# Gate in two runs, feed-forward interwoven with the attention phase's tail and the next phase's lead steps

## The chip, the cores and the metric

The kernel runs on one core of a Trainium2 chip. The metric is the device time of one execution in microseconds (us), as the median of several runs. TensorE is the matmul engine, VectorE (DVE), ScalarE (ACT) and GpSimd (POOL) work on tiles, and the queue of SyncE (SP) issues nearly all DMAs.

## The reference, cut to what matters

```python
x = x + attention_a(layernorm(x))        # x: 32 items x 256 tokens x 128, 16 heads of 8
x = x + ffn(layernorm(x))
x = x + attention_b(layernorm(x))
x = x + ffn(layernorm(x))

def ffn(x, gate_w, down_w, down_b, up_w, up_b):
    pooled = x.mean(axis=1)                              # one row per item
    gate = softmax(pooled @ gate_w.T)                    # 8 experts
    top_w, top_i = top_k(gate, 2);  top_w /= top_w.sum() + 1e-8
    h = gelu(x @ down_w[top_i].T + down_b[top_i]) * top_w
    return sum over the two experts of (h @ up_w[top_i].T + top_w * up_b[top_i])
```

The gate of an item needs the mean over that item's tokens alone. Items never mix, neither in the attention nor in the feed-forward.

## The kernel before, in words

x stays in SBUF for the whole run (32 items of two 128-token tiles). There are four blocks in a row, each ended by all engines: attention a, feed-forward a, attention b, feed-forward b.

**Attention** is a pipeline over items. Step n (from -6 to 34) works on several items at once. With 8 slots p = 0..7 (pairs of heads) it does: statistics of item n+6 and of item n-2 on VectorE (L351, L360); the normalisation of items n+5 and n-3 on GpSimd (L326 to L335, transposed on TensorE in L582, copied on ScalarE in L463 and L465; the second is the input of the feed-forward, `normT`, with its sum over tokens in `pooled`); queries and keys of item n+4 (L546, L438 to L441), split into bf16 parts on GpSimd (L298 to L304), bounced through DRAM by SP (L289, L292); reading the stacks of item n+3 back from DRAM (L271, L273) and its values (L565, L450); scores for the row maximum of item n+2 (L504, `max_side`) with the maximum itself on VectorE (L379, `nmax`); scores again with the maximum subtracted for item n (L521, `exp_side`), the exponential on ScalarE (L418); the weighted values (L486, `weigh`; the fourth quarter belongs to the step after); for item n-1 the transposes, division, transposes and output projection (L429, L558, L395, L574, L456, L592), added to x in the next step (L368). A step does only what is live: steps -6 to -3 are light, steps -2 and -1 have no exponentials, steps 30 and 31 no `max_side`, and steps 32, 33 and 34 only carry the last items through their chains. One PSUM bank, `m_bank`, is shared by all the small products; `fill_m` makes TensorE wait for the last reader before each new use.

**Feed-forward** begins with the gate for all 32 items at once (L709 to L740): one matmul, then a serial chain of small VectorE instructions with one exponential on ScalarE and three visits to TensorE. SP moves the two chosen indices per item into `index`. Then items run in turn, n = -2..33: for item n+2 ScalarE and GpSimd copy the two chosen halves of the down weights (`wd`, L790, L694), ScalarE and VectorE scale the two halves of the up weights (`wu`, L792, L759); every four items each of these engines reads four expert numbers into registers; TensorE does down (L818) for item n, ScalarE the Gelu (L783), TensorE bias and up (L825, L833) for item n-2, and VectorE adds to x (L752). In feed-forward a the steps -6, -5, -4 and -3 of attention b are put between items, each as a whole, after items 13, 17, 21 and 25 of the emission; attention b then begins at step -2. In feed-forward b SP stores each item.

All order is fixed by hand: every engine has its own in-order instruction list, with semaphores between them.

Of the kernel before, what the change touches and what calls it, by code (L numbers as in the profile page):

```python
# [13 lines left out]
P = 128  # L14
# [38 lines left out]
def build(nc, x_dram_in, attn_w, attn_b, gate_w, down_w, down_b, up_w, up_b, tail_c, ident_c, iota_c, pick_c, out):  # L53
    ctx = ExitStack()
    with ctx:
# [61 lines left out]
        weight = sb("weight", [P, ITEMS])  # L117
        hotT = sb("hotT", [EXPERTS, TOP + 3, ITEMS])
        biasd = sb("biasd", [P, ITEMS])
# [4 lines left out]
        biasu_parts = sb("biasu_parts", [3 * ITEMS, WIDTH], BF16)  # L124
        pick = sb("pick", [3 * ITEMS, ITEMS], BF16)
        index = sb("index", [1, ITEMS * TOP], U32)
# [21 lines left out]
        banks = [ring[i][:, a, :] for i in range(3) for a in range(2)]  # L148
        t_bank, o_bank = banks[2:4], banks[4:6]
        values_bank = ctx.enter_context(nc.psum_tensor("values_bank", [P, 512], FP32))  # L150
        m_bank = ctx.enter_context(nc.psum_tensor("m_bank", [P, 512], FP32))

# [6 lines left out]
        with nc.Block() as block:  # L159
# [27 lines left out]
            @block.gpsimd  # L187
            def _(pool):
                nc.gpsimd.memset(minus_half[:, :, :], -0.5)
                for i in range(2):  # L190
# [10 lines left out]
        def attention(name, w, bias, masked):  # L201
# [29 lines left out]
            m_reader = [None]  # L231

            def one_step(emit, n):

                emit(n, n % RING, lambda k: 0 <= n + k < ITEMS, lambda k: (n + k) // 2)

            def steps(engine, emit, first):
                for n in range(first, ITEMS + BACK):
                    one_step(emit, n)
# [4 lines left out]
            def pair_of_scores(n, p):  # L244

                return ring[2 * (n * PAIRS + p) % 3]
# [8 lines left out]

            def sync_program(sp):

                sp.wait_ge(tail_in, 4 * 16 if masked else 2 * 4 * 16)

                def step(n, r, live, half):  # L260
# [34 lines left out]
            def gpsimd_program(pool):  # L295
# [10 lines left out]
                def step(n, r, live, half):  # L306
                    if live(1):
# [10 lines left out]
                    if live(5) or live(-3):  # L318
# [11 lines left out]
                        if norm_steps(n) > 2:  # L330
                            pool.wait_ge(xyT_done, norm_steps(n - 2))
                        for m, item in ((0, n + 5), (1, n - 3)):
# [5 lines left out]
                    if live(4):  # L338

                        i = (r + 4) % 2  # L340
                        pool.wait_ge(qk32_ready, (n + 4) + 1)
                        if live(2):
                            pool.wait_ge(bounced[(r + 2) % 2], half(2) * 96 + 96)
                        split(qk32[i][:, :, :], rest[i][:, :, :], parts[i][:, 0], parts[i][:, 1], parts[i][:, 2],
                              hi_ready, rest_done, mid_ready, parts_ready, n + 4)
                return step

            def vector_program(dve):
# [5 lines left out]
                def aggregate(n, item, i, m, raw_d, mv_d):  # L354

                    dve.wait_ge(raw_d, item + 1)
                    if norm_steps(n - 1) > 0:
                        dve.wait_ge(xy_ready, norm_steps(n - 1))
                    for t in range(TILES):
# [3 lines left out]
                def step(n, r, live, half):  # L363
                    if live(-2):
# [5 lines left out]
                    for p in range(PAIRS):  # L370
                        if live(2):

                            i = (r + 2) % 2
                            if p == 0 and live(0):
                                dve.wait_ge(mparts_ready, n + 1)
                            dve.wait_ge(s_done, (n + 2) * PAIRS + (p + 1))
                            src = pair_of_scores(n, p)[:, :, :].rearrange("p x (t k) -> p x t k", t=TILES)
                            dst = nmax[i][:, :, :].rearrange("p t (x j) -> p x t j", x=2)[:, :, :, p]
                            nc.vector.tensor_reduce(dst, src, axis=AX.X, op=ALU.max, negate=True).then_inc(max_done, 1)  # L379
                        if p == 2 and live(6):  # L380

                            for c, (start, _) in enumerate(CHUNKS):
                                if masked and n + 6 == start:
                                    dve.wait_ge(x_in[c], 16)
                            stats(n + 6, r % 2, raw_done)
                        if p == 3 and live(-1):

                            dve.wait_ge(on_done, (n - 1) + 1)
                            if live(-2):
                                dve.wait_ge(oT2_done, (n - 2) + 1)  # L390
                            both = m_bank[:, :].rearrange("p (m w) -> p m w", w=32)[:, :, 0:IN_SHARE * SUMS]
                            both = both.rearrange("p m (g e) -> p m g e", g=IN_SHARE)
                            nc.vector.reciprocal(rsum[:, :, :], both[:, :, :, HEAD]).then_inc(rsum_done, 1)
                            dve.wait_ge(rsum_done, (n - 1) + 1)
                            nc.vector.tensor_tensor(o[:, :, :].rearrange("p t (m g d) -> p (t m) g d", g=IN_SHARE, d=HEAD),  # L395
# [512 lines left out]
```

## Time and profile before

| what | value |
|---|---|
| median of 3 runs (lowest, highest) | 1039.98 us (1037.24, 1041.08) |
| profiled execution: own time, span of the trace | 1038.88 us, 1037.0 us |
| busy: TensorE, VectorE, ScalarE, GpSimd | 913.8, 788.4, 759.8, 595.9 us |
| mean granted TensorE clock, share of full | 0.965 |
| DMA traffic | 131.64 MB, 127 GB/s mean |

The span runs from the first to the last instruction of the trace. A busy time is the sum of an engine's instructions. Since the four blocks have different limits, the table says little on its own: the stretches between the attention steady states have to be read one by one.

### The profile page before, as it was taken

How to read it: one execution, taken by the hardware profiler on the slowest of the kernel's cores; microseconds unless marked ns; L12 is line 12 of the kernel's file. 1: busy time of each engine (PE TensorE's matmuls, PEld its weight loads, DVE VectorE, ACT ScalarE, POOL GpSimd, SP SyncE). 2: the span in 40 equal slices, each digit the busy share in tenths (PEclk: the TensorE clock that was granted, in tenths of full speed). 3: DMA queues.
4: the chain of work that ended last, by engine and by line, in shares of the span. 5: the costliest groups of instructions: out<-in, count | busy, mean ns of one | idle time of the engine just before them, and what ended most of it. 6: DMA issues, size and time to landing. Idle time of an engine off the chain costs nothing. (4 is left out here: it accounts for less than half of the span.)

```text
span 1037.0 us, 27550 instructions
## 1 busy us (share of the span) xinstructions
PE 913.8 (88%) x10204; PEld 519.3 (50%) x10204; DVE 788.4 (76%) x1398; ACT 759.8 (73%) x1324; POOL 595.9 (57%) x1011
## 2 busy tenths in 40 slices
PE   2379999999999999984876999999999999998577
PEld 1235555555555555442753455555555555554266
DVE  0388888888888888843448899899999999885244
ACT  1147888888888888783752888888888888888466
POOL 4555666666666666422355566666666666643211
PEclk9989999999999999997897999999999999999779
DMA  8545555455554544300035554544555545540023
GB/s 238 169 148 145 147 144 145 144 150 142 145 152 145 144 142 151 107 3 21 2 104 157 151 154 140 151 150 149 143 151 151 147 146 144 156 129 3 1 59 106
DMA packets 140516, 131.64 MB, mean 127 GB/s; under 512 B 9880, under 2 KB 121888, under 8 KB 140256
## 3 DMA queue, kind: packets, MB, share of 16 engines
q1 hardware_dynamic: 139312, 128.49, 42.6%
q8 instruction: 82, 1.34, 0.6%
q10 hardware_dynamic: 1072, 1.40, 0.5%
q14 instruction: 50, 0.41, 0.1%
HBM read 73.75 MB, written 55.57 MB: 125 GB/s over the span
## 5 line engine op out<-in xcount | busy, mean ns | idle before, releaser
L379 DVE TENSOR_REDUCE nmax<-ring 128x4 f32<-128x1024 f32 x512 | 607.8, 1217 | 74.1 <-PE ring L504 73.8
L418 ACT ACTIVATE probs<-ring 128x1024 f32<-128x1024 f32 x512 | 510.3, 1027 | 49.7 <-PE ring L521 46.4
L486 PE MATMUL values_bank<-probs,values 128*32 128x256 f32 x4096 | 274.1, 385 | 5.9 <-ACT probs L418 5.9
L504 PE MATMUL ring<-k_stack,q_stack 64*128 64x256 bf16 x2048 | 201.7, 278 | 42.9 <-DMA k_stack<-scratch 23.1
L335 POOL TENSOR_SCALAR xy<-x,mv,rstd 128x128 f32<-128x128 f32 x256 | 202.1, 800 | 8.7
L521 PE MATMUL ring<-q_stack,k_stack 64*128 64x256 bf16 x2048 | 187.4, 273 | 0.7 <-DVE nmax L379 0.4
L486 PEld LDWEIGHTS values_bank<-probs,values 128*32 128x32 f32 x4096 | 106.8, 109 | 90.4 <-issue 23.4
L298 POOL TENSOR_SCALAR mparts<-nmax 128x32 bf16<-128x32 f32 x64 | 13.9, 218 | 230.2 <-DVE nmax L379 230.2
L504 PEld LDWEIGHTS ring<-k_stack,q_stack 64*128 64x128 bf16 x2048 | 74.6, 95 | 139.0 <-ACT probs L418 67.3
L521 PEld LDWEIGHTS ring<-q_stack,k_stack 64*128 64x128 bf16 x2048 | 83.9, 95 | 75.4 <-issue 36.9
L450 ACT COPY values<-m_bank 128x128 f32<-128x128 f32 x128 | 29.0, 278 | 81.6 <-PE m_bank L565 81.6
L304 POOL TENSOR_TENSOR parts<-rest,parts 128x512 bf16<-128x512 f32 x64 | 74.4, 1162 | 5.3
L300 POOL TENSOR_TENSOR rest<-qk,parts 128x512 f32<-128x512 f32 x64 | 74.1, 1158 | 5.3
L368 DVE TENSOR_TENSOR x<-x,m_bank 128x256 f32<-128x256 f32 x64 | 26.9, 421 | 65.5 <-PE m_bank L592 65.5
L328 POOL TENSOR_TENSOR rstd<-varp,minus_half 128x4 f32<-128x4 f32 (+1 forms) x80 | 72.9, 911 | 6.7
L582 PE MATMUL m_bank<-ident,xy 128*128 128x128 f32 x256 | 47.3, 298 | 30.5 <-POOL xy L335 26.3
L351 DVE BATCH_NORM_STATS2 raw<-x 128x6 f32<-128x128 f32 x256 | 60.8, 279 | 15.0 <-PEq L159 14.9
L818 PE MATMUL ring<-normT,wd 128*128 128x256 f32 x128 | 45.1, 442 | 15.9 <-issue 7.7
L298 POOL TENSOR_SCALAR parts<-qk 128x512 bf16<-128x512 f32 x64 | 39.9, 624 | 27.2 <-ACT qk L439 17.9
L694 POOL COPY wd<-down_sb 128x64 f32 x64 | 14.7, 243 | 68.2 <-PE ring L818 52.0
L429 ACT COPY oT<-values_bank 128x512 f32<-128x512 f32 x64 | 37.5, 586 | 21.2 <-PE values_bank L486 21.2
L582 PEld LDWEIGHTS m_bank<-ident,xy 128*128 128x128 f32 x256 | 27.2, 144 | 48.7 <-POOL xy L335 18.5
(99 smaller groups left out, 1028.9 us busy)
## 6 DMA issues: line engine op xcount, KB each, us to landing
q_stack<-scratch SPq DMA_DIRECT2D x128, 256.0 KB
k_stack<-scratch SPq DMA_DIRECT2D x128, 256.0 KB
scratch<-parts SPq DMA_DIRECT2D x128, 192.0 KB, 2.5
scratch<-parts SPq DMA_DIRECT2D x128, 128.0 KB, 2.5
scratch<-parts SPq DMA_DIRECT2D x128, 64.0 KB, 3.1
out<-x SPq DMA_DIRECT2D x32, 128.0 KB, 1.8
q_stack<-maxT SPq DMA_DIRECT2D x128, 12.0 KB
scratch<-in_tail SPq DMA_DIRECT2D x8, 128.0 KB, 3.3
```

What stands on the lines that cost most here:

```text
L298: nc.gpsimd.tensor_scalar(hi, src, 1.0, 0.0, ALU.mult, ALU.add).then_inc(hi_done, 1)
L300: nc.gpsimd.tensor_tensor(tmp, src, hi, ALU.subtract).then_inc(rest_d, 1)
L304: nc.gpsimd.tensor_tensor(lo, tmp, mid, ALU.subtract).then_inc(lo_d, 1)
L328: nc.gpsimd.tensor_tensor(rstd[i][:, both, :], varp[i][:, both, :], minus_half[:, both, :], ALU.pow).then_inc(rstd_done, 1)
L335: last = nc.gpsimd.tensor_scalar(xy[i][:, m, t, :], x[:, item * TILES + t, :], mv[i][:, m, t, 0:1], rstd[i][:, m, t:t + 1], ALU.subtract, ...
L351: last = nc.vector.bn_stats(raw[i][:, t, :], x[:, item * TILES + t, :])
L379: nc.vector.tensor_reduce(dst, src, axis=AX.X, op=ALU.max, negate=True).then_inc(max_done, 1)
L418: nc.scalar.activation(probs[g % 2][:, c:c + 2, :, :], pair_of_exps(n, p)[:, :, :].rearrange("p x (k q) -> p x k q", k=TILES), ACT.Exp).th ...
L486: last = nc.tensor.matmul(values_bank[32 * c:32 * (c + 1), a * TOKENS:(a + 1) * TOKENS], values[item % RING][:, k, PER_GROUP * g + c, :], ...
L504: last = nc.tensor.matmul(pair_of_scores(n, p)[:, a, t * TOKENS:(t + 1) * TOKENS], q_stack[z][rows, p, t * P:(t + 1) * P], k_stack[z][rows ...
L521: last = nc.tensor.matmul(pair_of_exps(n, p)[:, a, k * TOKENS:(k + 1) * TOKENS], k_stack[r][rows, p, k * P:(k + 1) * P], q_stack[r][rows, ...
L582: last = nc.tensor.transpose(m_bank[:, at:at + P], xy[(r + 5) % 2][:, m, t, :], ident[:, :])
```

## The change

Each attention step can now be emitted slot by slot. The attention block ends after step 31. Steps 32, 33 and 34 are put between the items of the feed-forward that follows (`BEFORE`). The gate is computed in two runs: the first, for items 0 to 27, has its pieces between the slots of attention step 31; the second, for all 32 rows, of which items 28 to 31 are used, between the items 9 to 14 of the feed-forward (`GATE`). For the two runs `weight`, `biasd`, `biasu_parts` and `index` exist twice. The gate's products go to `m_bank` in place of the ring banks. Steps -6 to -2 of attention b are spread in pieces over items 8 to 32 of feed-forward a (`AFTER`); attention b then begins at step -1. The table of Gelu is no longer preloaded. The scores of steps before 0 use one ring bank pair (step -2 of b) or two (the others) where they used three. Three small memsets come into the set-up, and SP waits for the constant rows at step -3, not before the first step.

```diff
-            def sync_program(sp):
-                sp.wait_ge(tail_in, 4 * 16 if masked else 2 * 4 * 16)
+                    if n == -3:
+                        sp.wait_ge(tail_in, 4 * 16 if masked else 2 * 4 * 16)
...
-                return ring[2 * (n * PAIRS + p) % 3]
+                i = n * PAIRS + p
+                return ring[2 * i % 3 if i >= 0 else i % 2 if i >= SINGLE else 0]
...
+            SINGLE = -2 * PAIRS if masked else -PAIRS
...
-                    elif i - 3 >= -2 * PAIRS:
-                        pe.wait_ge(max_done, (i - 3) + 2 * PAIRS + 1)
+                    elif i < SINGLE and i - 1 >= -2 * PAIRS:
+                        pe.wait_ge(max_done, (i - 1) + 2 * PAIRS + 1)
+                    elif i != 1 and i - 2 >= max(SINGLE, -2 * PAIRS):
+                        pe.wait_ge(max_done, (i - 2) + 2 * PAIRS + 1)
...
+            def tensor_logits(pe):
+                fill_m(pe, dve_g, 1)
+                pe.wait_ge(yT_ready, rows)
...
+            def tensor_transposes(pe):
+                fill_m(pe, dve_g, HOT_T)
+                pe.wait_ge(dve_g, MIXED)
...
+            def tensor_biases(pe):
+                fill_m(pe, dve_g, BIASD + 1)
+                pe.wait_ge(dve_g, HOT_T)
...
+            programs = {"tensor": {1: tensor_logits, 5: tensor_transposes, 7: tensor_biases}, "scalar": {3: scalar_exps},
+                        "vector": {2: vector_best, 4: vector_top, 6: vector_weights, 8: vector_biases},
+                        "sync": {4: sync_index}, "gpsimd": {}}
...
+        EARLY = ITEMS - RING
+        def run(phase, first, gate):
+                for n in range(first, ITEMS):
+                    for p in range(PAIRS):
+                        phase["slot"](step, n, p)
+                        piece = gate["programs"][kind].get(p + 1)
+                        if n == ITEMS - 1 and piece:
+                            piece(engine)
...
+            BEFORE = {-2: (32, 0, 3), 0: (32, 3, 4), 1: (32, 4, 7), 2: (32, 7, 8), 4: (33, 0, 8), 7: (34, 0, 8)}
+            GATE = {9: (1, 2), 10: (2, 3), 11: (3, 4), 12: (4, 5), 13: (5, 7), 14: (7, 9)}
+            AFTER = {8: (-6, 0, 8), 10: (-5, 0, 3), 14: (-5, 3, 8), 15: (-4, 0, 3), 16: (-4, 3, 6), 17: (-4, 6, 8),
+                     18: (-3, 0, 3), 19: (-3, 3, 6), 20: (-3, 6, 8), 21: (-2, 0, 1), 23: (-2, 1, 2), 25: (-2, 2, 3),
+                     27: (-2, 3, 6), 30: (-2, 6, 7), 32: (-2, 7, 8)}
+            down_bank = [ring[2][:, i, 0:TOKENS] for i in range(2)]
+            up_bank = [values_bank[:, 0:TOKENS], ring[1][:, 0, 0:TOKENS]]
...
-                    nc.scalar.preload_act_table(ACT.Gelu)
...
-        run(phase_a, -6)
-        feed_forward("fa", False, phase_b)
-        run(phase_b, -2)
-        feed_forward("fb", True)
+        run(phase_a, -6, gate_a[0])
+        feed_forward("fa", phase_a, gate_a, phase_b, False, x_given[0])
+        run(phase_b, -1, gate_b[0])
+        feed_forward("fb", phase_b, gate_b, None, True, x_given[1])
```

## Rows read from the trace of the kernel before

**Rows 1.** Busy time in stretches: start:end, length, each engine's busy us, clock, DMA.

```profile
100.00:440.00 340.00, 332.42 (x4002) 182.98 (x4002) 300.55 (x490) 282.11 (x469) 224.65 (x363) 1.00 0.49 142
...
470.70:482.90 12.20, 4.58 (x32) 2.34 (x32) 3.00 (x12) 2.90 (x9) 4.98 (x8) 0.79 0.00 0
482.90:491.50 8.60, 1.91 (x14) 1.26 (x14) 5.06 (x27) 1.68 (x4) 0.76 (x4) 0.50 0.21 62
491.50:541.60 50.10, 41.38 (x242) 33.18 (x242) 22.12 (x81) 35.84 (x103) 21.47 (x48) 0.93 0.18 54
541.60:564.00 22.40, 12.17 (x86) 6.49 (x87) 19.83 (x25) 4.47 (x10) 13.53 (x23) 0.83 0.53 155
...
969.00:981.80 12.80, 5.54 (x32) 2.87 (x33) 2.70 (x12) 2.48 (x9) 4.98 (x8) 0.65 0.00 0
...
990.30:1034.80 44.50, 38.11 (x224) 31.02 (x224) 19.73 (x65) 33.10 (x96) 6.73 (x28) 0.93 0.31 90
```

**Rows 2.** Timeline, last step of attention a: start, length, engine, line, count, idle before.

```profile
464.90 0.39 PE L521 MATMUL ring<-q_stack,k_stack 64*128 64x256 bf16 x4
...
469.39 0.40 ACT L465 ACTIVATE normT<-m_bank 128x256 f32<-128x256 f32 x1
...
471.17 1.07 PE L486 MATMUL values_bank<-probs,values 128*32 128x256 f32 x16 [0.48 <-ACT probs L418]
472.30 0.59 ACT L429 COPY oT<-values_bank 128x512 f32<-128x512 f32 x1 [1.19 <-PE values_bank L486]
```

**Rows 3.** Timeline of gate a, from the exponential to the first weights.

```profile
484.25 1.28 ACT L773 ACT_TABLE_LOAD   x1
484.33 0.15 DVE L713 RECIPROCAL tsum<-esum 32x1 f32<-32x1 f32 x1 [0.53 <-ACT e L772]
...
487.20 0.18 PEld L800 LDWEIGHTS ring<-ident,wide 32*128 32x128 f32 x1 [4.05 <-DVE mix L726]
...
489.68 0.19 DVE L733 COPY biasd<-ring 128x32 f32<-128x32 f32 x1 [1.25 <-PE ring L808]
...
491.49 0.24 ACT L790 COPY wd<-down_sb 128x64 f32 x1 [5.96 <-DVE biasu_mid L737]
```

**Rows 4.** Timeline of ScalarE in feed-forward b: its start, and its steady state.

```profile
990.33 0.24 ACT L790 COPY wd<-down_sb 128x64 f32 x1 [5.99 <-DVE biasu_mid L737]
...
1001.62 0.24 ACT L790 COPY wd<-down_sb 128x64 f32 x1 [0.93 <-issue]
1001.89 0.40 ACT L792 ACTIVATE wu<-up_sb,weight 64x128 f32 x1
1002.31 0.47 ACT L783 ACTIVATE hT<-ring,biasd 128x256 f32<-128x256 f32 x1
```

**Rows 5.** Timeline around feed-forward a's end: lead steps of attention b.

```profile
527.18 0.70 PE L818 MATMUL ring<-normT,wd 128*128 128x256 f32 x2 [1.93 <-POOL wd L694]
...
532.03 0.45 ACT L450 COPY values<-m_bank 128x128 f32<-128x128 f32 x2 [0.80 <-PE m_bank L565]
...
542.77 3.49 DVE L379 TENSOR_REDUCE nmax<-ring 128x4 f32<-128x1024 f32 x3 [0.76 <-PE ring L504]
...
553.57 0.60 SPq L271 DMA_DIRECT2D q_stack<-scratch  x1
...
560.71 1.28 ACT L418 ACT_TABLE_LOAD   x1
...
564.02 0.61 PE L504 MATMUL ring<-k_stack,q_stack 64*128 64x256 bf16 x4 [3.41 <-DMA k_stack<-scratch]
...
565.09 1.02 ACT L418 ACTIVATE probs<-ring 128x1024 f32<-128x1024 f32 x1 [3.10 <-PE ring L521]
```

**Rows 6.** The page's groups: line, engine, operation, count, busy us, mean ns, idle before.

```profile
L335 POOL TENSOR_SCALAR xy<-x,mv,rstd 128x128 f32<-128x128 f32 x256 | 202.1, 800 | 8.7
...
L304 POOL TENSOR_TENSOR parts<-rest,parts 128x512 bf16<-128x512 f32 x64 | 74.4, 1162 | 5.3
...
L298 POOL TENSOR_SCALAR parts<-qk 128x512 bf16<-128x512 f32 x64 | 39.9, 624 | 27.2 <-ACT qk L439 17.9
```

More of the change, by code:

```diff
@@ L198, in _, with attention @@
                         nc.gpsimd.memset(of_group(r, g)[:, :, :, at:at + 1], 1.0)
-        def attention(name, w, bias, masked):
+        def attention(name, w, bias, masked, earlier=None, x_given=None):
             BACK = 3
@@ L229, in attention, with slot @@
             wq, wk, wv, wo = (w[:, i * WIDTH:(i + 1) * WIDTH] for i in range(4))
[L231 to L239, printed above, removed]
+            def slot(emit, n, p):
+                emit(n, p, n % RING, lambda k: 0 <= n + k < ITEMS, lambda k: (n + k) // 2)
             def tiles_of(item):
@@ L304, in split, with step @@
                     nc.gpsimd.tensor_tensor(lo, tmp, mid, ALU.subtract).then_inc(lo_d, 1)
-                def step(n, r, live, half):
-                    if live(1):
+                def step(n, p, r, live, half):
+                    if p == 0 and live(1):
                         i = (r + 1) % 2
@@ L361, in aggregate, with step @@
                     last.then_inc(mv_d, 1)
-                def step(n, r, live, half):
-                    if live(-2):
+                def step(n, p, r, live, half):
+                    if p == 0 and live(-2):
                         dve.wait_ge(wo_done, (n - 2) + 1)
@@ L604, in run, with steps @@
+        EARLY = ITEMS - RING
+        def run(phase, first, gate):
+            def steps(kind, engine):
+                step = phase["programs"][kind](engine)
+                for n in range(first, ITEMS):
[4 more added lines that the diff above has]
+                            piece(engine)
             with nc.Block() as block:
@@ new lines, in feed_forward, with of_item, steps @@
+            down_bank = [ring[2][:, i, 0:TOKENS] for i in range(2)]
+            up_bank = [values_bank[:, 0:TOKENS], ring[1][:, 0, 0:TOKENS]]
+            def of_item(item):
+                return gate_of[item >= EARLY], int(item >= EARLY)
+            def steps(kind, engine, emit):
+                old = before["programs"][kind](engine)
+                new = after["programs"][kind](engine) if after else None
+                for n in range(-AHEAD, ITEMS + BACK):
+                    if n in BEFORE:
+                        of_step, first, end = BEFORE[n]
+                        for p in range(first, end):
+                            before["slot"](old, of_step, p)
+                    for turn in range(*GATE.get(n, (0, 0))):
+                        if turn in gate_of[1]["programs"][kind]:
+                            gate_of[1]["programs"][kind][turn](engine)
+                    if after and n in AFTER:
+                        of_step, first, end = AFTER[n]
+                        for p in range(first, end):
+                            after["slot"](new, of_step, p)
+                    emit(n, n % RING, lambda k: 0 <= n + k < ITEMS)
@@ L835, in step @@
                             last.then_inc(up_done, 1)
-                    steps(pe, step, ahead_steps(pe, "tensor"))
+                    steps("tensor", pe, step)
                 @block.sync
                 def _(sp):
-                    sp.wait_ge(dve_g, WHICH)
-                    for k in range(TOP):
-                        sp.dma_start(index[0:1, k * ITEMS:(k + 1) * ITEMS], which[:, k:k + 1]).then_inc(index_in, 16)
-                    sp.wait_ge(index_in, 16 * TOP)
                     if not store:
@@ L856, in _ @@
+                    steps("sync", sp, step)
+                    if store:
                         sp.wait_ge(stored, 16 * ITEMS)
+        x_given = [sem("fa_x_ready"), sem("fb_x_ready")]
         phase_a = attention("a", wa, True, True)
-        phase_b = attention("b", wb, False, False)
-        run(phase_a, -6)
-        feed_forward("fa", False, phase_b)
-        run(phase_b, -2)
-        feed_forward("fb", True)
+        phase_b = attention("b", wb, False, False, phase_a, x_given[0])
+        gate_a, gate_b = ([gates(f"g{name}{i}", i, rows, phase["yT_ready"]) for i, rows in enumerate((EARLY, ITEMS))]
+                          for name, phase in (("a", phase_a), ("b", phase_b)))
```

588 lines of the change are left out of this document (300 added, 288 removed).

## The prediction

> **What bounds the kernel now.** I read the busy times in stretches first, and look for the stretches that are neither steady state. In the steady attention (100 to 440 us) TensorE is busy 332.42 of 340 us: that part is full, and the change leaves its instructions and their order alone [rows 1]. What lies between the two attentions, and behind the second, is not full. From 470.70 to 482.90 the three tail steps run with 4.58 us of TensorE and 2.90 us of ScalarE in 12.20; the gate takes 8.60 us with the clock at half speed; in feed-forward a ScalarE does 35.84 of 50.10 us; the lead steps -2 and -1 take 22.40 us, mostly VectorE [rows 1]. The same at the end: tail 12.80, gate about 8.5 (from 981.80 to the first weights at 990.33), feed-forward 44.50 [rows 1, 4]. The tail and the gate are chains of waits, one engine at a time, 42 us in all. That is what the change attacks.
>
> Then I read the timelines of these stretches, to see who sets the pace in each. In the feed-forward it is ScalarE: `wd`, `wu`, Gelu follow each other without a gap, 1.055 us an item by start to start, and each four items have a gap of 0.93 us for the expert numbers, so 5.27 us for four items [rows 4]. **Whatever ScalarE gets in addition in a feed-forward, lengthens it by that time.** GpSimd and VectorE have room there (feed-forward b: 6.73 and 19.73 us busy of 44.50 [rows 1]).
>
> **The attention's last step with the gate's first run.** The anchor is the last quarter of `weigh` for item 31, at 471.17, first work of step 32 before and after [rows 2]. Step 31 gets the gate's pieces in the in-order lists. The exponential of the gate stands behind those of slots 0 to 2 on ScalarE, and ends some 0.3 us after slot 4's scores (464.90 [rows 2]), at about 465.2. From there the VectorE chain to the last `mix` takes 487.17-484.33 = 2.84 us [rows 3], to 468.0. TensorE waits for it behind slot 4, and behind it stands the second quarter of `weigh`, which ran right after 464.90+0.8: with 0.6 us of transposes it comes about 2.9 us late, and so do slot 5's scores and ScalarE's exponentials of slots 5 to 7. Then the piece with the biases (turn 7) has to wait for the reader of `m_bank`, ScalarE's `normT` of that step, which stands behind the exponentials of slots 5 and 6 (469.39+0.40+0.2 before [rows 2], 3 us later now). Before, the third quarter of `weigh` and slot 7's scores ran during that time; now they follow it: biases 0.8 (between its half-clock row, about 1.2, and half of that), `weigh` 1.07, scores 0.4, exponential 1.0. Late in all: 5.1 us. Bounds: 2 (ScalarE's backlog covers most) and 8.
>
> **What goes.** From `weigh` to the first `wd`: before 491.49-471.17 = 20.3 us in a, and in b, where the same `weigh` opens the stretch at 969.0, 990.33-969.0 = 21.3 us [rows 1 to 4]. After: 5.1 late, `weigh` and semaphore 1.13, `oT` 0.59, then the expert numbers 0.93: 7.75 us. Gain 12.6 in a, 13.5 in b. What is late next is ScalarE itself.
>
> **What the feed-forwards get, both of them.** On ScalarE: `onT` 0.4, three `normT` at 0.4 with a read-out of 0.2 each, together 2.2 (from 469.39 [rows 2]); the second gate's exponential 0.4; table loads. The load of Gelu was hidden in the gate's chain (484.25 [rows 3]). Now the first Gelu brings it into the line, 1.28 us, of which 0.25 lie in the wait for the first down product: 1.0. The second gate's exponential brings two more, back and forth, 2.56. Waits: step 32's transposes and projection need each other's results at distances of one item, 0.8 us; TensorE waits at item 13 for the VectorE chain of 2.84 us, begun at item 11, and at item 14 for the copies behind it: 1.6 us beyond the two items that ScalarE is ahead. For the better: the clock. It stood at 0.50 in the gate and the first items of the feed-forward ran slowly [rows 1]; without the idle stretch they start at full clock, -1.0 us (bounds 0 and -2). Steps 33 and 34 have their GpSimd work (0.9+1.6 each [rows 6]) spaced by three items: hidden, and if not, up to 2 us each. Index and second weights are wanted only from item 26: hidden. Sum 2.2+0.4+1.0+2.6+0.8+1.6-1.0 = **7.6 us** for each feed-forward. Bounds 4 and 14.
>
> The Trainium skill (ScalarE: Activation LUTs, What ACT_TABLE_LOAD costs) gives about 1.28 us for the load and another 1.38 us for a drain with each switch of set. The load is the same here; for the drain no row speaks, since behind both loads ScalarE waits for others anyway. By that rule three switches would cost 4.1 us more in each feed-forward, and the sum would be 8 us worse.
>
> **What feed-forward a gets besides.** It took 50.05 us to the end of its items, b 44.0, so whole steps -6 to -3 cost 6 us now [rows 1]. After, steps -6 to -2: on ScalarE four `xnT` at 0.4, three `qk` at 0.6, two `values` at 0.45 [rows 5] = 4.2 us. On GpSimd each of steps -4 and -3 has 0.9+1.6 for the normalisation and 2 x 0.62+2 x 1.16 for the parts [rows 6], 6.3 us, and both now fall on items 15 to 20: 12.6 us and six `wd` at 0.4 make 15; ScalarE needs about 10 there, GpSimd is 2.3 ahead: 2.7 us late. That GpSimd can hold up the items, a row shows: 1.93 us at 527.18 [rows 5]. Step -2 has eight `nmax` of 1.16 us (3.49 for three [rows 5]) on VectorE, 9.3 us over items 21 to 32, with 0.7 of its own work for each item and the register reads: 22 us against ScalarE's 18.5; and since these scores have one bank pair, slots 3 to 5, emitted together at item 27, let TensorE wait for two `nmax` in a row, some 3 us. The two overlap: 4 us. Together 10.9, less 6 = **4.9 us more**. Bounds 1 and 12.
>
> **The lead steps after it.** Before, 22.40 us from the block's start to step 0, of which step -1 began at 551.6; the end of that time is set by a DMA: the reads for item 2 were issued at 553.57 and the scores had them at 564.02, 10.4 us later [rows 1, 5]. After, step -2 is gone from here, item 2's parts are ready before the feed-forward ends, and SP issues that read at once. It then lands at +0.8+10.4 = 11.2 us from the end of feed-forward a; VectorE's step -1, eight `nmax` and statistics, needs 10.1 and, with two bank pairs where there were three, 0.8 more, and one us of starting. I take 13.2 (0.8 block start, 11.6, 0.8), bounds 11.2 and 16. Gain 22.5-13.2 = **9.3 us**. At the start of attention a the two pairs cost the same 0.8, largely under the waits for the reads: 0.5. Memsets and the moved wait of SP: nothing, they lie under the loads of the first 14 us.
>
> **Sum.** a: 12.6-7.6-4.9+9.3 = 9.4. b: 13.5-7.6 = 5.9. Start -0.5. Together 14.8 us. The profiled execution had 1037.0 us of span and 1.9 around it, 1038.88; it becomes 1024.1. The median shown is 1.1 higher: **1025 us**. Steady attention and final store are taken as unchanged.
>
> **Rivals.** *A, better hidden.* The late 5.1 in step 31 is mostly covered, as ScalarE has exponentials in hand, and step -2 fits beside the items. With the lower bounds (2 for 5.1 twice, 5 for 7.6 twice, 1.5 for 4.9): 15 us more, 1010. For: every engine but ScalarE has room. Against: the lists are in order, and TensorE's waits stand in front of work that ScalarE needs.
> *B, the waits multiply.* Each wait for `m_bank` inside the feed-forward stops TensorE, ScalarE runs dry, and it adds to ScalarE's own time instead of overlapping. Both feed-forwards at 13 for 7.6, a's further 4.9 at 12, step 31 at 8 for 5.1 twice: 10.8+7.1+5.8 = 24 us less gain, so 1049, slower than before. It decides from some 15 us beyond my sum on. For: one lead step now brings waits of 1.93 us (TensorE, 527.18) and 0.80 (ScalarE, 532.03) [rows 5]. Against: pieces are small and set apart.
> *C, about half of B*: 12 of those 24 us are lost, 1037.
> *D, a switch of the table costs more than its row.* Its upper bound is the 3.1 us that pass between the load's end at 561.99 and the next exponential [rows 5], which waits for scores there. At half of it, 1.5 us for each of the six loads, 9 us: 1034. For: no row has work waiting behind a load. Against: the load at 560.71 starts without a pause. The skill's rule above is this case, at 1033.
> *E, the change does not do what it says.* The items of the feed-forward are held by the tail's chains, since the steps 32 to 34 stand in the same in-order lists, ahead of items 0 to 7: the tail is moved and not hidden. Then 12.2+12.8 us come back, less the 2.2+0.8 charged for them twice: 19 us, 1044. Against: the pieces lie one to three items apart, and their longest part, 2.5 us of GpSimd, is shorter.
>
> **Chances.** Forecast (1016 to 1032) 0.55; A 0.2; D 0.07; C 0.08; E 0.03; B 0.07. The range takes A's centre and goes to C: 1009 to 1038. A difference of 0.5% (5.2 us) is about what this measurement can tell from none: faster 0.82 (forecast, A, D), same 0.11 (C, E), slower 0.07 (B).
>
> **What would show it.** Right: the last `weigh` of item 31 about 5 us behind its old place with TensorE waits for `mix` and for `normT` in step 31; first `wd` some 8 us behind 471; three table loads in each feed-forward with 1.28 us between ScalarE's items; feed-forwards of about 52 and 61 us from first `wd` to last up; step 0 of b about 13 us after feed-forward a. Wrong: a first `weigh` delay under 3 us, no gap for the loads, item gaps at 15 to 20 and at 27 missing, or a wait for the stacks of item 1 or 2 longer than before.

## The result, and the profile after

| | before | after |
|---|---|---|
| median (lowest, highest), 4 runs each | 1040.33 us (1037.24, 1041.08) | 1052.32 us (1050.28, 1055.79) |
| ratio, 95% interval | | 1.0133 (1.0116 to 1.015) |
| profiled execution: own time, span | 1038.88, 1037.0 us | 1050.78, 1048.9 us |
| mean granted clock | 0.965 | 0.964 |

The kernel became 12 us slower where 15 us of gain were forecast. The time lies outside the range, and beside rival B (1049). Chips differ a little (the kernel before has medians from 1038.78 to 1040.33 us below), so each experiment is compared with the runs of the kernel before that were made beside it.

First the busy times in stretches of the kernel after (start:end, length, each engine's busy us with its instructions, clock, DMA). They are cut by stage, finer than [rows 1]:

```profile
61.00:463.00 402.00, 386.77 (x4643) 211.12 (x4642) 344.72 (x557) 329.12 (x538) 252.97 (x412) 1.00 0.47 136
463.00:478.60 15.60, 10.86 (x111) 5.29 (x105) 6.28 (x32) 8.46 (x14) 0.02 (x1) 0.78 0.01 1
...
481.30:492.60 11.30, 7.09 (x26) 5.42 (x26) 2.98 (x13) 7.13 (x19) 4.10 (x12) 0.70 0.07 20
492.60:502.50 9.90, 8.96 (x60) 7.43 (x61) 6.07 (x27) 8.14 (x25) 5.76 (x12) 1.00 0.01 2
502.50:519.70 17.20, 12.05 (x56) 9.21 (x55) 8.88 (x40) 9.18 (x23) 4.47 (x13) 0.70 0.01 1
519.70:528.80 9.10, 6.62 (x44) 5.40 (x43) 6.50 (x17) 6.91 (x22) 8.57 (x15) 1.00 0.40 120
528.80:562.40 33.60, 21.80 (x129) 15.86 (x129) 17.70 (x34) 12.18 (x36) 9.12 (x19) 0.80 0.35 102
562.40:572.90 10.50, 5.88 (x45) 2.73 (x46) 9.74 (x15) 2.97 (x6) 6.95 (x12) 0.86 0.51 155
...
1010.00:1025.30 15.30, 10.32 (x49) 7.77 (x49) 7.98 (x35) 8.24 (x21) 1.19 (x5) 0.67 0.17 48
1025.30:1046.10 20.80, 18.11 (x119) 15.07 (x117) 9.84 (x31) 15.88 (x47) 2.85 (x12) 1.00 0.34 99
```

The reader sees two kinds of stretch. Where attention is in its steady state (61 to 463) nothing is lost, and little where only items run, or items with light pieces: 492.6 to 502.5 and 1025.3 to 1046.1 hold the full clock (1.00) with ScalarE busy for about four fifths; from 519.7 to 528.8 the clock is full too, and GpSimd has no room left (8.57 of 9.10). In the others, step 31 (463.0 to 478.6), the first items with step 32, the items with the second gate (502.5 to 519.7 and 1010.0 to 1025.3) and the items with step -2 (528.8 to 562.4), TensorE is busy for 63 to 70% and the clock is at 0.67 to 0.80. Idle time that stood in one block before is now cut up and placed among the work.

The change, from piece to piece (starts in the two traces):

| piece | before | after | forecast | measured |
|---|---|---|---|---|
| start, attention a | | | +0.5 | +1.04 |
| last `weigh` of item 31, a | 471.17 | 478.58 | +5.1 | +6.4 |
| from it to the first `wd` | 20.32 | 2.73 | -17.7 | -17.6 |
| feed-forward a, to the last up product | 50.06 | 81.09 | +12.5 | +31.0 |
| from there to step 0 of b | 22.5 | 10.5 | -9.3 | -12.0 |
| attention b up to step 31 | | | 0 | +0.9 |
| last `weigh` of item 31, b | 969.14 | 985.51 | +5.1 | +6.6 |
| from it to the first `wd` | 21.19 | 3.35 | -18.6 | -17.8 |
| feed-forward b | 43.98 | 57.28 | +7.6 | +13.3 |

Measured, they give 11.9 us, which is 1048.9-1037.0. Of the 1.04 us at the start 0.72 stand already at the first matmul (19.24 against 18.52 us); experiments below with the same set-up have it between 18.57 and 19.34, so that part is no effect of the change. What was to go went; what came instead was too much, 18.5 us of it in feed-forward a and 5.7 in b. Where inside: I counted the start of each item's Gelu from the first `wd`. In b the difference grows at a few places only:

| Gelu of item | before b | after b | after a |
|---|---|---|---|
| 0 | 1.6 | 2.9 | 2.7 |
| 5 | 8.8 | 13.9 | 14.1 |
| 10 | 15.1 | 20.7 | 20.8 |
| 15 | 22.8 | 36.0 | 37.9 |
| 20 | 29.1 | 42.3 | 47.1 |
| 26 | 36.5 | 49.7 | 66.5 |
| 27 | 38.6 | 51.8 | 74.7 |
| 31 | 42.7 | 56.0 | 79.6 |

In b: 1.3 for the table load, 3.8 more up to item 5 (step 32), 0.5 up to item 10 (steps 33 and 34, hidden as forecast), 7.6 from 10 to 15 (the second gate), then nothing. In a the same, and from item 15 on 41.7 us where b takes 20.0; the gap before item 21 alone is 9.2, that before item 27 is 8.2.

The waits of TensorE in feed-forward a (line waited at, who released it, us in total, times, longest):

```profile
PE ring L521 <- DMA k_stack<-scratch: 6.5, 1, 6.5
PE ring L521 <- DVE nmax L399: 4.1, 2, 2.8
PE m_bank L637 <- DVE mix L685: 3.8, 1, 3.8
PE m_bank L598 <- ACT onT L477: 3.0, 1, 3.0
```

All but that for `nmax` (two) are single waits, with TensorE's whole queue behind it. In the timeline (start, length, engine, line, tiles, count, and the idle time before):

```profile
469.18 0.22 PE L637 MATMUL m_bank<-ident,wide 32*128 32x32 f32 x1 [2.72 <-DVE mix L685]
...
473.71 0.42 PE L648 MATMUL m_bank<-hotT,downb_sb 8*64 8x32 f32 x4 [1.35 <-ACT normT L486]
...
474.73 1.94 PE L501 MATMUL values_bank<-probs,values 128*32 128x256 f32 x16
...
477.25 1.02 ACT L439 ACTIVATE probs<-ring 128x1024 f32<-128x1024 f32 x1 [3.59 <-PE ring L538]
...
504.04 1.28 ACT L654 ACT_TABLE_LOAD   x1
505.34 0.30 ACT L654 ACTIVATE e<-logit,nbest 32x8 f32<-32x8 f32 x1
505.55 0.18 ACT L654 ACTIVATION_READ_ACCUMULATOR e<-logit,nbest 32x1 f32 x1
505.75 1.28 ACT L858 ACT_TABLE_LOAD   x1
507.04 0.47 ACT L858 ACTIVATE hT<-ring,biasd 128x256 f32<-128x256 f32 x1
...
508.72 0.28 PE L637 MATMUL m_bank<-ident,wide 32*128 32x32 f32 x1 [3.79 <-DVE mix L685]
...
509.20 1.22 PE L880 MATMUL ring<-normT,wd 128*128 128x256 f32 x2
...
511.59 0.47 ACT L858 ACTIVATE hT<-ring,biasd 128x256 f32<-128x256 f32 x1 [2.46 <-PE ring L900]
...
525.24 0.69 SPq L279 DMA_DIRECT2D q_stack<-scratch  x1
...
534.72 0.61 PE L521 MATMUL ring<-k_stack,q_stack 64*128 64x256 bf16 x4 [6.46 <-DMA k_stack<-scratch]
535.25 1.22 PE L880 MATMUL ring<-normT,wd 128*128 128x256 f32 x2
...
537.64 0.47 ACT L858 ACTIVATE hT<-ring,biasd 128x256 f32<-128x256 f32 x1 [8.26 <-PE ring L900]
```

Read it from TensorE's wait to ScalarE's: `mix` holds TensorE for 3.79 us, and ScalarE then idles for 2.46, and for 1.22 and 1.61 more in the two items behind; the stacks hold TensorE for 6.46, and ScalarE idles for 8.26. The price is that of ScalarE. At the stacks it is more than TensorE's wait, because the matmuls behind that wait run at half clock: the down products at 535.25 take 1.22 us for two, as at 509.20 behind `mix`, against 0.70 at 527.18 [rows 5]. In step 31 `weigh` takes 1.94 us at 474.73 against 1.07 [rows 2].

### The profile page after: what moved, and what is told of

Its sections match the earlier page's. It is cut to its first block and busy times, and to the rows that moved or that the text cites. A ratio compares the mean times of both kernels' runs of the same rounds, so it can differ in the third digit from the quotient of the medians.

```text
span 1048.9 us, 27756 instructions
## 1 busy us (share of the span) xinstructions
PE 929.5 (89%) x10232; PEld 528.0 (50%) x10232; DVE 803.3 (77%) x1452; ACT 765.9 (73%) x1332; POOL 594.7 (57%) x1014
## 5 line engine op out<-in xcount | busy, mean ns | idle before, releaser
L501 PE MATMUL values_bank<-probs,values 128*32 128x256 f32 x4096 | 277.2, 388 | 3.4 <-ACT probs L439 2.7
L306 POOL TENSOR_SCALAR mparts<-nmax 128x32 bf16<-128x32 f32 x64 | 13.9, 218 | 233.6 <-DVE nmax L399 227.2
L334 POOL TENSOR_SCALAR varp<-mv 128x4 f32<-128x4 f32 (+1 forms) x80 | 15.7, 197 | 71.4 <-POOLq L734 39.2
L880 PE MATMUL ring<-normT,wd 128*128 128x256 f32 x128 | 48.5, 466 | 7.0 <-issue 4.2
```

The costliest lines, as they stand in the source:

```text
L501: last = nc.tensor.matmul(values_bank[32 * c:32 * (c + 1), a * TOKENS:(a + 1) * TOKENS], values[item % RING][:, k, PER_GROUP * g + c, :], ...
L880: nc.tensor.matmul(down_bank[r % 2], wd[r][:, :, :].rearrange("p a b -> p (a b)"), normT[:, n, :], start=True, stop=True).then_inc(down_do ...
```

## The experiments

Each kernel is the one after with the edit shown, or an experiment before it with one edit more. W is the theory that waits of TensorE in the in-order lists make the loss. "After, a / b" below are the lengths of feed-forward a and b in the trace, 81.09 and 57.28 in the kernel after. Feed-forward b is the same code in that kernel and in e1, e2 and e4, and has 57.28 to 58.95 there: such a length is good to about 1.7 us.

| label | median us (runs) | kernel before, us | ratio, 95% | a / b |
|---|---|---|---|---|
| e1_lead2_out | 1046.52 (5) | 1038.87 | 1.0082 (1.0054 to 1.0111) | 63.65 / 57.50 |
| e2_lead2_late | 1044.44 (5) | 1038.87 | 1.0062 (1.0041 to 1.0082) | 71.74 / 58.95 |
| e3_gate2_none | 1036.57 (10) | 1038.87 | 0.9978 (0.996 to 0.9996) | 71.95 / 49.64 |
| e4_gate1_at6 | 1044.39 (5) | 1038.87 | 1.0054 (1.0032 to 1.0077) | 81.08 / 57.84 |
| e6_gate2_noexp | 1049.91 (4) | 1040.01 | 1.0109 (1.0082 to 1.0137) | 80.26 / 56.0 |
| e7_gate2_spaced | 1047.86 (4) | 1040.01 | 1.0083 (1.0062 to 1.0104) | 79.98 / 54.78 |
| e9_all_late | 1031.16 (4) | 1040.01 | 0.9926 (0.9904 to 0.9948) | 69.26 / 53.67 |
| e10_before_spaced | 1023.46 (4) | 1040.01 | 0.984 (0.982 to 0.9861) | 64.75 / 51.21 |
| e11_preload_moved | 1019.45 (5) | 1038.78 | 0.982 (0.9803 to 0.9837) | 64.75 / 49.64 |
| e12_lead2_out_all | 1023.81 (4) | 1038.78 | 0.9859 (0.9844 to 0.9874) | 55.91 / 49.98 |
| e13_exp_earlier | 1019.73 (5) | 1038.78 | 0.9821 (0.9807 to 0.9836) | 64.61 / 49.82 |

**Step -2 out of the feed-forward (e1_lead2_out).** It runs at the start of attention b as before the change, with the three bank pairs.

```diff
-                     18: (-3, 0, 3), 19: (-3, 3, 6), 20: (-3, 6, 8), 21: (-2, 0, 1), ... 32: (-2, 7, 8)}
+                     18: (-3, 0, 3), 19: (-3, 3, 6), 20: (-3, 6, 8)}
-        run(phase_b, -1, gate_b[0])
+        run(phase_b, -2, gate_b[0])
-                return ring[2 * i % 3 if i >= 0 else i % 2 if i >= SINGLE else 0]
+                return ring[2 * (n * PAIRS + p) % 3]
```

> Step -2 of attention b is taken out of feed-forward a and runs whole at the start of attention b, as before the change; the scores of steps before 0 have three bank pairs again. The rest is the changed kernel (1052.3 us; span 1048.9). Theory W (in-order waits): in the changed kernel items 21 to 33 of feed-forward a take 34 us where bare items take some 15, so the step costs 19 there and saves 12 behind it. Without it: feed-forward a some 62 us from first wd to last up (81 in the changed kernel), lead steps 22 us again, first step of a 1 us earlier: 1052.3-7-1 = 1044 us. Rival V (volume: the step's work costs what it costs wherever it stands): feed-forward a shorter by just the 12 us that come back behind it, 1051 us.

Feed-forward a is 17.4 us shorter, and the way from its last up product to the next exponential is 24.1 us, where it was 11.8. Net 4.2 us of span. So step -2 inside cost more than it saved. What is left of feed-forward a is 6.2 us longer than b (63.65 and 57.50), as in the kernel before (50.06 and 43.98, 6.1 us): spreading steps -6 to -3 cost nothing more in sum, and step -2 is what made feed-forward a so much longer than b.

**Step -2 at the end of it (e2_lead2_late).** The slots stand behind items 26 to 33, one each.

```diff
-                     18: (-3, 0, 3), 19: (-3, 3, 6), 20: (-3, 6, 8), 21: (-2, 0, 1), 23: (-2, 1, 2), 25: (-2, 2, 3),
-                     27: (-2, 3, 6), 30: (-2, 6, 7), 32: (-2, 7, 8)}
+                     18: (-3, 0, 3), 19: (-3, 3, 6), 20: (-3, 6, 8), 26: (-2, 0, 1), 27: (-2, 1, 2), 28: (-2, 2, 3),
+                     29: (-2, 3, 4), 30: (-2, 4, 5), 31: (-2, 5, 6), 32: (-2, 6, 7), 33: (-2, 7, 8)}
```

> The same instructions as the changed kernel; step -2's eight slots stand at items 26 to 33, one each, in place of items 21, 23, 25, 27 (three), 30, 32. Theory W: TensorE's 6.5 us wait for the stack of item 0 (and the half clock behind it) goes, since the read lands some 5 items earlier than wanted; the two waits for nmax at item 27 go as well, but VectorE has eight nmax of 1.2 us in eight items of 1.3: some 3 us come back. 1052.3-6 = 1046 us; no wait of TensorE for k_stack in feed-forward a. Rival V: the volume of VectorE and ScalarE sets the time, no change or slower by 1 to 3 us (all of it crowded at the end), 1052 to 1055 us.

The waits of TensorE from 480 to 552 in its trace:

```profile
PE m_bank L637 <- DVE mix L685: 3.8, 1, 3.8
PE m_bank L598 <- ACT onT L477: 3.0, 1, 3.0
PE ring L521 <- DVE nmax L399: 2.4, 5, 1.2
```

The wait for the stacks is gone, that for `nmax` is 2.4 us in five pieces, feed-forward a is 9.35 us shorter, and the step is still inside. From the Gelu of item 20 to that of item 21 it is 1.1 us where it was 9.2, to that of item 27 5.2 where it was 8.2. The first slot stands 5 items later and the three slots of item 27 stand apart; the work is the same: the place was most of the fault. Against e1 the step still costs 8.1 us inside. The waits for `mix` and `onT` stand as they were.

**The second gate left out (e3_gate2_none).** Items 28 to 31 take the experts and weights of items 24 to 27, so that part of the computation is missing.

```diff
-            GATE = {9: (1, 2), 10: (2, 3), 11: (3, 4), 12: (4, 5), 13: (5, 7), 14: (7, 9)}
+            GATE = {}
+            col = lambda i: i if i < EARLY else i - RING
```

> The second run of the gate is left out in both feed-forwards; items 28 to 31 take the experts and weights of items 24 to 27 (that part of the computation is changed). Theory W: five items with the gate take 15.3 us in feed-forward b where bare ones take 7.1, and about as much more in a: 8 us each, 1052.3-16 = 1036 us, first wd at the same place. Rival P (the prediction's price, 0.4+2.6+1.6 each): 1052.3-9 = 1043 us.

Both feed-forwards are shorter, by 9.1 and 7.6 us. The 7.6 us in b are just what the table of Gelu starts had between items 10 and 15. The wait for the stacks stays (7.6 us where it was 6.5). This kernel is also where a second gate that costs nothing would end, at about the time of the kernel before.

**The first gate's visits to TensorE joined (e4_gate1_at6).** Transposes and biases both stand behind slot 5, one slot later than the transposes stood and one earlier than the biases.

```diff
+            if run_of == 0:
+                programs["tensor"] = {1: tensor_logits, 6: tensor_both}
+                programs["vector"] = {2: vector_best, 4: vector_top, 6: vector_both}
```

> Only the first run of the gate is moved inside attention step 31: its transposes come behind slot 5 (were behind slot 4), its biases right behind them (were behind slot 6, waiting for normT); VectorE's pieces follow. Theory W: TensorE issues weigh and scores of slot 5 before it waits, so ScalarE keeps working; the wait for normT is gone. The last weigh of item 31 comes 2 us late in place of 6.4 and 6.6: 1052.3-9 = 1043 us. Rival: the gate's chain itself has to fit into the step and only changes place, last weigh still 5 to 6 us late: 1051 us.

The last `weigh` comes at 472.98 in a (478.58 in the kernel after), and at 975.58 in b (985.51): 5.6 us in a and 4.3 more in b. Of the 6.4 us that step 31 was late, 0.8 are left.

**No table loads for the second gate (e6_gate2_noexp).** ScalarE copies the logits where it took their exponential, so the weights of items 28 to 31 are others.

```diff
-                nc.scalar.activation(e[of_run, :], logit[of_run, :], ACT.Exp, bias...
+                nc.scalar.activation(e[of_run, :], logit[of_run, :], ACT.Identity if run_of else ACT.Exp, bias...
```

> The changed kernel with the second gate's exponential replaced by a plain copy with bias on ScalarE (the gate of items 28 to 31 is computed wrongly): same instructions and waits, but no load of the Exp table and none back to Gelu in the feed-forwards. Leaving the second gate out altogether gave 7.6 us in feed-forward b and 9.1 in a. Theory W: two loads of 1.28 us each are in ScalarE's line, the rest is TensorE's wait for the VectorE chain (3.8 us) with the half clock behind it; the chain starts 1.3 us earlier: some 2.6 to 3.5 us less in each feed-forward, 1052.5-6 = 1046 us. Rival D (a switch costs more than its row, 2.8 us each): 5.5 us or more less in each, 1041 us.

Two loads of 1.28 us gone in each feed-forward, and they are shorter by 0.8 and 1.3 us only, less than such lengths can tell. Its timeline shows the reason:

```profile
504.95 0.30 ACT L654 ACTIVATE e<-logit,nbest 32x8 f32<-32x8 f32 x1
...
505.38 0.15 DVE L671 RECIPROCAL tsum<-esum 32x1 f32<-32x1 f32 x1
...
507.97 0.21 DVE L685 SCALAR_TENSOR_TENSOR mix<-hot,wt,mix 32x8 f32<-32x8 f32 x1
508.33 0.28 PE L637 MATMUL m_bank<-ident,wide 32*128 32x32 f32 x1 [2.51 <-DVE mix L685]
...
511.20 0.47 ACT L858 ACTIVATE hT<-ring,biasd 128x256 f32<-128x256 f32 x1 [3.90 <-PE ring L900]
```

The chain on VectorE, 2.8 us from 505.38 to 508.18, sets when TensorE goes on. ScalarE's Gelu of item 13 starts at 511.20 in place of 511.59; the loads had lain mostly beside that chain, and ScalarE idles for 3.90 us where it idled for 2.46. My size for W (1046) missed, and D, which asked for 5.5 us or more in each, is refuted.

**The second gate's last pieces later (e7_gate2_spaced).**

```diff
-            GATE = {9: (1, 2), 10: (2, 3), 11: (3, 4), 12: (4, 5), 13: (5, 7), 14: (7, 9)}
+            GATE = {9: (1, 2), 10: (2, 3), 11: (3, 4), 12: (4, 5), 15: (5, 7), 18: (7, 9)}
```

> The changed kernel with the second gate's last pieces later: transposes and weights at item 15 (were 13), biases at item 18 (were 14). Nothing is left out. Theory W: TensorE no longer waits 3.8 us for mix and keeps its clock, ScalarE's table loads stay: about 4 of 8 us come back in each feed-forward, 1052.5-8 = 1044 us. Rival V (volume of the gate's instructions on VectorE and ScalarE): 0 to 2 us, 1051 us. In a the pieces fall among steps -4 and -3, so less may come back there.

1.1 us less in a and 2.5 in b, of the 9.1 and 7.6 that the second gate costs: the value lies between the two expectations. TensorE's wait for `mix` is gone, 3.8 us in each. In b a wait of 2.8 us for ScalarE's `wd`, behind the two table loads, has come in its place; in a there is one too, and the stacks still hold TensorE for 4.5 us. So this wait was partly beside work of ScalarE, and only the part beyond came back.

**All three, and the load of Gelu's table at the end of the attention (e9_all_late).** e2, e4 and e7 together, and one line:

```diff
+                if kind == "scalar":
+                    nc.scalar.preload_act_table(ACT.Gelu)
```

> Three edits together: step -2's slots at items 26 to 33 (alone -8 us), first gate behind slot 5 (alone -8), second gate's last pieces at items 15 and 18; and in addition the Gelu table is preloaded at the end of the attention blocks, behind the last exponential, where ScalarE waits for weigh anyway. Theory W: the waits are separate and add up: 1052.5-8-8-8-2.6 = 1026 us, faster than before by 13. Rival: behind each wait the next one comes forward (table loads, GpSimd's parts, VectorE's nmax), half of it stays: 1037 us.

The spans of e2, e4 and e7 lie 7.9, 10.3 and 4.6 us under that of the kernel after. Added, they give 1026.1; e9 has 1028.3. The trace of e4 is its fastest run, 4 us under its median; by the medians (7.9, 7.9 and 4.5 under 1052.32) the sum is 1032.0, and e9 has 1031.16. The savings add up, within some 2 us, and the load added nothing to them: what it gives in the feed-forward (the first Gelu 1.6 us behind `wd` where it was 2.7) goes at the block's end, where it stands last on ScalarE and all engines wait for it.

```profile
475.45 1.28 ACT L744 ACT_TABLE_LOAD   x1
...
477.03 1.07 PE L501 MATMUL values_bank<-probs,values 128*32 128x256 f32 x16 [1.72 <-PEq L746]
```

That wait is 0.73 us in e4, which has the same step 31 and no load (0.40 in the kernel after, whose step 31 ends otherwise).

**Step 32 spaced out (e10_before_spaced).** Each piece of step 32 that uses another's result stands an item later, and steps 33, 34, the gate and step -6 one item later too.

```diff
-            BEFORE = {-2: (32, 0, 3), 0: (32, 3, 4), 1: (32, 4, 7), 2: (32, 7, 8), 4: (33, 0, 8), 7: (34, 0, 8)}
+            BEFORE = {-2: (32, 0, 3), 0: (32, 3, 4), 1: (32, 4, 6), 2: (32, 6, 7), 3: (32, 7, 8), 5: (33, 0, 8), 8: (34, 0, 8)}
-            GATE = {9: (1, 2), 10: (2, 3), 11: (3, 4), 12: (4, 5), 15: (5, 7), 18: (7, 9)}
+            GATE = {10: (1, 2), 11: (2, 3), 12: (3, 4), 13: (4, 5), 16: (5, 7), 19: (7, 9)}
```

> As the kernel with all edits, with the attention's tail further apart in the feed-forward: step 32's slots 6 and 7 one item later each, step 33 at item 5 (was 4), step 34 at 8 (was 7), the gate's pieces and step -6 one item later. Theory W: TensorE waits 3.0 us for onT at item 1 since ScalarE has the Gelu load and item 0 first; the preload and the distance take 2 to 3 us from each feed-forward: 2 to 4 us below the kernel with all edits, 1023 us. Rival V: no difference between the two.

It brought 7.7 us of the medians against e9, more than was expected of the step alone: 4.5 in feed-forward a, 2.5 in b. In a the first Gelus start at 1.6, 3.1, 5.0, 7.1 and 8.1 us, where e9 had 1.6, 4.8, 7.7, 9.8 and 12.0. Up to item 5, where only step 32 differs, it is 2.6 us in a and 3.0 in b; the rest of the gain belongs to the other pieces that moved.

**The load moved to the start of the feed-forward (e11_preload_moved).** It is ScalarE's first instruction there.

```diff
                     experts = [None]
+                    nc.scalar.preload_act_table(ACT.Gelu)
```

> As the kernel with the spaced tail (1023.5), but the Gelu table is loaded as the first instruction of ScalarE in each feed-forward block, not as the last of the attention block. In that kernel TensorE waits 2.0 us at the block's start before the last weigh (0.40 in the changed kernel), as all engines end the block together and ScalarE's load of 1.28 us belongs to it. Theory: behind the start it lies in ScalarE's wait for that weigh, so the weigh comes 1.3 us earlier in each phase and hT(0) stays 1.6 us behind the first wd: 1021 us. Rival: the load pushes oT by what weigh gained, no difference, 1023.5 us.

```profile
463.00:473.10 10.10, 7.16 (x87) 3.35 (x85) 6.17 (x30) 7.17 (x13) 0.00 (x0) 1.00 0.01 2
475.85:540.60 64.75, 49.80 (x310) 38.46 (x310) 39.90 (x127) 42.22 (x118) 32.41 (x69) 0.95 0.26 74
```

```profile
473.10 1.28 ACT L859 ACT_TABLE_LOAD   x1 [0.28 <-PEq L744]
...
473.13 1.07 PE L501 MATMUL values_bank<-probs,values 128*32 128x256 f32 x16 [0.73 <-PEq L744]
...
474.39 0.59 ACT L450 COPY oT<-values_bank 128x512 f32<-128x512 f32 x1
...
475.85 0.24 ACT L876 COPY wd<-down_sb 128x64 f32 x1 [0.88 <-issue]
```

The load lies under the last `weigh`, and costs nothing: the first `wd` stands 2.72 us behind that `weigh`, 2.73 in the kernel after, which has no load there. The clock is 1.00 from 463 us to the end of step 31 and 0.95 over feed-forward a, where the kernel after had 0.78 and 0.81. This version beats both kernels: 1019.45 us, 1.8% under the kernel before (0.9803 to 0.9837), with the same pieces in other places and the load ahead of the first items. The 4.0 us under e10's median are not all the load's: against the kernel before, e10 has 0.982 to 0.9861, which overlaps. The traces show TensorE's wait at the two block ends shorter by 1.3 and 0.9 us (2.02 and 1.51 in e10, 0.73 and 0.56 here). The rest is not explained; e10's step 31 in a ran at 0.87 where this one has 1.00.

**Step -2 out again, from the good version (e12_lead2_out_all).** e11 with the edit of e1.

```diff
-                     18: (-3, 0, 3), 19: (-3, 3, 6), 20: (-3, 6, 8), 26: (-2, 0, 1), ... 33: (-2, 7, 8)}
+                     18: (-3, 0, 3), 19: (-3, 3, 6), 20: (-3, 6, 8)}
-        run(phase_b, -1, gate_b[0])
+        run(phase_b, -2, gate_b[0])
```

> As e11, but step -2 of attention b whole at the start of attention b, and three bank pairs for all scores before step 0. Tells whether the step is worth its place in the feed-forward once it is set late. Theory W: with late slots it still costs some 10 us in the feed-forward (VectorE's eight nmax) and saves 12 behind it; and the three pairs give 1 us back at the start: within 2 us of e11, 1020 to 1023 us. Rival (the overlap of step -2 is where the gain is): 10 us slower, 1031 us.

Feed-forward a is 8.8 us shorter, and the way to the next exponential is 23.1 us instead of 12.4. So step -2 inside now costs less than it saves, 1.7 us of span and 4.4 of the medians, where it had cost 4.2 more than it saved in the kernel after. That is more than the first expectation allowed (1023) and far from the rival (1031).

**The first gate's exponential earlier (e13_exp_earlier).** e11 with that piece behind slot 1 instead of slot 2.

```diff
+                programs["scalar"] = {2: scalar_exps}
```

> As e11, with the first gate's exponential one slot earlier on ScalarE (behind slot 1 of step 31, was behind slot 2). VectorE's chain then begins behind its own division of slot 3 instead of behind the exponential, some 0.4 to 0.7 us earlier. Theory W: TensorE's wait for mix and all behind it shrink by that, 0.5 us in each phase, 1020 us. Rival: no difference to e11, since VectorE is what the chain waits for.

1019.73 against 1019.45: no difference that this can tell. The edit hardly moved the chain: from the logits' matmul to `wide`, the first matmul behind `mix`, it is 6.83 us in a and 6.73 in b, where e11 has 6.88 and 6.87. An earlier end of the chain was therefore not tried; the exponential was not what held it.

## Why the prediction was wrong, point by point

- **From `weigh` to the first `wd`**: right, 2.73 and 3.35 us for 2.65. The tail and the gate did leave their place, so rival E (not hidden at all) is out: steps 33 and 34 cost at most 0.5 us together.
- **Step 31**: right in kind and near in size. Both waits that were named are there (2.72 for `mix`, 1.35 for `normT`), and 6.4 us late for 5.1. The part missing is the clock: `weigh` behind them took 1.94 us, where the sum had 1.07.
- **The load of the table**: 1.28 us, and no more. ScalarE's items stand right behind it (505.75 and 1.28, next start 507.04), at all six loads. D's mechanism does not exist here. The Trainium skill (ScalarE: Activation LUTs, What ACT_TABLE_LOAD costs) gives about 1.28 us for the load, as measured, and 1.38 us more for a drain, which none of these six loads shows.
- **The lead steps after feed-forward a**: right in its mechanism, 10.5 us for 13.2, and 0.7 under the lower bound. SP issued the read for item 2 at 563.39, 1.0 us behind the last up product (562.40), and the scores had it at 572.90, 9.5 us later where the sum took 10.4 and 1.2 more for VectorE.
- **What the feed-forwards get, 7.6 each**: wrong, 13.3 in b. Step 32 was priced at 0.8 us of waits, and 1.0 of ScalarE's own for `onT` and a `normT`, and cost 3.8 up to item 5. The second gate was priced at 0.4+2.6+1.6 = 4.6 and cost 7.6. That "they start at full clock, -1.0 us" did not come: over the first 11.3 us of feed-forward a the clock was 0.70, as in the kernel before, here behind the waits of steps 31 and 32.
- **Feed-forward a's further 4.9 us**: the step that failed. It measured 31.0-13.3 = 17.7, the largest miss of the sum (12.8 us). The prediction priced step -2 by VectorE's work and two `nmax` waits, and never asked when the stacks of item 0 would be there: it put that wait at nothing. Slot 0 of step -2 stands at item 21, the read's issue was at 525.24, three items ahead, and the scores had it at 534.72: 9.5 us. Moving the step later took 8.1 us out of this one gap (e2), and with the step out altogether feed-forward a is 17.4 us shorter (e1). A row for such a read was at hand, 10.4 us from issue to scores [rows 5], and I used it for item 2 after the feed-forward only.
- **The rule behind all of these**: the prediction took a wait of TensorE as lying beside ScalarE's work ("the two items that ScalarE is ahead"). At the stacks ScalarE went on for only 1.1 us after TensorE had stopped (529.39 against 528.26), and behind a wait TensorE needs longer for each item than ScalarE does: from 487.83 to 489.75 the down products came 1.92 us apart at half clock, against 1.055 of ScalarE [rows 4]. So that wait was paid in full and a little more: from the kernel after to e2 the waits for stacks and `nmax` fall by 8.2 us, and feed-forward a by 9.35. The wait for `mix` was not: of its 3.8 us in b, e7 got 2.5 back, since ScalarE had two table loads beside it. This was rival B, given 0.07; its 13, 12 and 8 us stand against 13.3, 17.7 and 6.4 measured, so that its 1049 is near partly because its misses offset. Rival A's 1010 is no sum of the stated lower bounds: it takes 5 and 1.5 us where they are 4 and 1, and with those it would be 1008, outside the range.

What was shown: step -2's places, which hold the stacks' wait and that for `nmax` together (e2), the second gate (e3), the two visits in step 31 (e4), step 32's distances up to item 5 (e10) and the end-of-block load (e9 against e11), each by its own kernel. What the half clock alone adds in the feed-forwards was not separated. For the end of step 31, e11's two phases do it: from the start of the second bias matmul to the next block the same instructions take 4.27 us in a, at a clock of 1.00, and 5.59 us in b, at 0.69. There the clock alone is 1.3 us.

## What to carry to other kernels

Interweaving a chain with in-order work pays only if every piece stands so far behind what it needs, a DMA's landing and another engine's chain included, that the shared engine does not wait; here the same pieces gave +1.3% or, in other places and with one table load ahead of the items, -1.8%. Price a wait of the shared engine at its full length plus the slower items behind it, and take off only what the pacing engine is shown to have of its own to do there, as the table loads here. For each moved step, list every transfer that it reads and compare its issue, plus the landing time of a row, with the new place.

## What the runs showed of the hardware, unexpected

**The half clock behind short waits.** Behind TensorE's waits of 3.0, 3.8 and 6.5 us in feed-forward a the granted clock was 0.50 (1.2 of 2.4 GHz) for 6.0, 10.0 and 4.6 us (485.5 to 491.5, 508.7 to 518.7, 534.7 to 539.3), with up to 1.92 us an item. Shorter waits have it at times: behind the same wait for `mix` in step 31 (2.72 and 2.71 us) `weigh` took 1.07 us in a and 1.93 in b.

**VectorE beside GpSimd.** `wu` on VectorE takes 0.27 us. With the parts of queries and keys now beside the items, some took four times that:

```profile
519.53 1.25 DVE L842 TENSOR_SCALAR wu<-up_sb,weight 64x128 f32 x1
519.54 1.16 POOL L358 TENSOR_TENSOR rest<-qk,parts 128x512 f32<-128x512 f32 x1
...
528.58 1.16 POOL L364 TENSOR_TENSOR parts<-rest,parts 128x512 bf16<-128x512 f32 x1
...
528.63 1.18 DVE L842 TENSOR_SCALAR wu<-up_sb,weight 64x128 f32 x1
```

In both cases `wu` ends just behind GpSimd's instruction beside it (0.08 and 0.07 us). Of all 64, the durations are (lowest, median and highest in ns):

```profile
L842 DVE TENSOR_SCALAR wu<-up_sb,weight x64: 245/274/1246, 480.5 to 1043.0; 64x128 f32 x64
```

The Trainium skill (SBUF — State Buffer, Who interferes with whom) says that VectorE's `tensor_scalar` can take both of its port pairs, one of which GpSimd shares, and that one of the two engines then holds the pair for its whole instruction while the other is blocked. These two rows agree with it: a `wu` of 0.27 us lasts as long as the 1.16 us instruction beside it. It cost little here: 22.0 us for all 64, where they took 17.4 before.

**A table load delays the end of a block.** With the load last on ScalarE (e9), the next block begins 1.60 us after ScalarE's last exponential in a; with the load behind the end (e11), 0.28 us after it. TensorE waits 1.72 and 0.73 us there. Behind the end, beside a 1.07 us `weigh`, it was free (e11).
